# Making and storing the outputs of seven batches between the last two passes of a software-pipelined transformer kernel

## The reference

```python
x = x + tanh(g_xattn) * xattn(layernorm(x), ctx, ctx, Wq, bq, Wk, bk, Wv, bv, Wo, bo)   # 16 heads of 8
x = x + tanh(g_ffn) * stack(layernorm(x), ...)
# stack:
for i in range(6):
    x = attn_layer(shift_tokens(x), ...) + x     # 16 heads of 64, rotary, windows of 32 tokens and the 32 before
    x = ffn_layer(shift_tokens(x), ...) + x      # norm, 128 -> 2 x 341, a * gelu(gate), 341 -> 128
```

## Time and profile before

| what | us |
|---|---|
| median of 3 runs | 2186.88 (2184.47 to 2193.87) |
| the profiled execution, its own time | 2175.77 |
| its span, first to last instruction | 2173.8 |
| TensorE busy | 1993.4 (92% of the span) |
| VectorE busy | 1612.6 (74%) |
| ScalarE busy | 1092.6 (50%) |
| GpSimd busy | 891.2 (41%) |

### The profile page before, as it was taken

One profiled execution on the slowest core, in us unless ns is written; L12 is line 12 of the kernel. 1 busy time (PEld: TensorE's weight loads), 2 busy tenths in 40 slices (PEclk: granted clock), 3 DMA queues, 4 the chain that ended last, 5 costly groups with the idle time before them and its releaser, 6 DMA issues.

```text
span 2173.8 us, 84521 instructions
## 1 busy us (share of the span) xinstructions
PE 1993.4 (92%) x35280; PEld 1294.1 (60%) x35280; DVE 1612.6 (74%) x3316; ACT 1092.6 (50%) x1911; POOL 891.2 (41%) x1166
## 2 busy tenths in 40 slices
PE   6988987789999999999999999999999999999995
PEld 2333332456666666666766666767676766666763
DVE  5565563667878788787878787878787878787872
ACT  2333333345555555555555555656565646464643
POOL 1000000444545555455545454545454646463540
PEclk9999999899999999999999999999999999999996
DMA  1000100455556555556555565555655556554550
GB/s 61 5 5 10 53 0 1 69 85 82 84 82 123 93 84 84 83 111 104 86 80 89 97 108 90 89 79 96 114 96 87 84 84 112 103 86 81 84 83 21
DMA packets 73218, 166.72 MB, mean 77 GB/s; under 512 B 16592, under 2 KB 23504, under 8 KB 72272
## 3 DMA queue, kind: packets, MB, share of 16 engines
q0 software_dynamic: 36864, 100.71, 34.0%
q1 hardware_dynamic: 36320, 65.55, 11.8%
HBM read 20.45 MB, written 1.05 MB: 10 GB/s over the span
## 4 chain that ended last, share of the span: by engine, by line
PE 54%; DVE 18%; DMA 14%; issue 9%; POOL 4%; ACT 1%; POOLq 0%; DVEq 0%; SPq 0%; ACTq 0%
DMA big<-big 13%; PE ps L948 12%; PE ps L983 8%; PE ps L871 6%; PE ps L959 5%; PE ps L1020 4%; DVE big L770 4%; DVE big L767 3%; PE ps L1037 3%; POOL big L452 3%; PE ps L1007 3%; PE ps L892 2%; DVE big L801 2%; PE ps L876 2%; DVE big L788 2%
## 5 line engine op out<-in xcount | busy, mean ns | idle before, releaser
L452 POOL DMA_DIRECT2D big<-big x768 | 607.5, 1494 | 66.8 <-DVE big L770 56.1
L948 PE MATMUL ps<-big,wn_sb 128*128 128x256 f32 x1536 | 394.4, 393 | 25.5 <-issue 15.0
L520 ACT ACTIVATE big<-ps 128x512 f32<-128x512 f32 x384 | 229.1, 597 | 331.8 <-PE ps L948 325.4
L948 PEld LDWEIGHTS ps<-big,wn_sb 128*128 128x128 f32 x1536 | 273.2, 190 | 103.6 <-issue 46.5
L778 DVE TENSOR_TENSOR big<-big,ps 128x512 f32<-128x512 f32 x384 | 243.2, 682 | 103.3 <-DMA big<-big 52.4
L533 ACT ACTIVATE big<-ps 128x512 f32<-128x512 f32 x192 | 114.7, 598 | 371.3 <-PE ps L983 371.3
L783 DVE TENSOR_REDUCE top<-ps 128x8 f32<-128x512 f32 x192 | 123.3, 684 | 202.8 <-PE ps L1007 202.8
L767 DVE TENSOR_TENSOR big<-ps,tab 128x512 f32<-128x512 f32 x384 | 257.9, 682 | 9.3 <-ACT big L520 9.3
L770 DVE TENSOR_TENSOR big<-ps,tab 128x512 f32<-128x512 f32 x384 | 257.6, 681 | 0.0
L443 POOL TENSOR_TENSOR big<-big 128x512 f32<-128x512 f32 x96 | 121.9, 1270 | 294.2 <-ACT big L537 294.2
L1091 PE MATMUL ps<-big,wo_sb 128*128 128x256 f32 x768 | 213.1, 380 | 2.2 <-issue 2.2
(11 more groups left out here) (146 smaller groups left out, 3219.1 us busy)
## 6 DMA issues: line engine op xcount, KB each, us to landing
big<-big POOLq DMA_DIRECT2D x768, 128.0 KB, 4.9
big<-big SPq DMA_DIRECT2D x96, 256.0 KB, 3.9
big<-big SPq DMA_DIRECT2D x96, 192.0 KB, 4.0
wn_sb<-in_wn SPq DMA_DIRECT2D x6, 1024.0 KB, 9.1
wn_sb<-in_wn SPq DMA_DIRECT2D x6, 512.0 KB, 4.7
wo_sb<-in_wo SPq DMA_DIRECT2D x6, 512.0 KB, 3.4
w_sb<-in_w SPq DMA_DIRECT2D x6, 341.0 KB, 2.9
w_sb<-in_w SPq DMA_DIRECT2D x6, 192.0 KB, 2.9
```

Of the source, the lines that this page charges most:

```text
L452: eng.dma_start(rot[to:to + 32, at:at + 4, :], src[32 * r:32 * r + 32], accum_op=ALU.add).then_inc(added[i], 16)
L520: eng.activation(sq[:, two, :], ps[:, i % 2, :].rearrange("p (a t) -> p a t", a=2), ACT.Square).then_inc(sq_d, 1)
L948: mm = eng.matmul(ps[:, k % 2, a * T:a * T + T], wn_sb[:, u * P:u * P + P], sT, start=True, stop=True)
```

## The change

One helper, `outputs(first, last)`, holds the output steps of PE, ACT and DVE. It is called twice: for batches 0 to 6 between pass 48 and pass 49, and for batch 7 behind pass 49. `otok` grows from two buffers to eight, so the copies on ACT no longer wait for stores. The wait of DVE for `fx` becomes 48 (batch 6 added) in the first call and stays at 49 in the second. The loop on SP is the same but for the buffer that it reads.

```diff
-        otok = view(2 * 2 * P, 2, 2, P)
+        otok = view(B * 2 * P, B, 2, P)
...
             body(0, L * B, L, False, True, True, False)
+            if outputs:
+                outputs(0, B - 1)
             body(1, L * B + 1, L, False, False, True, False)
...
+            if outputs:
+                outputs(B - 1, B)
...
             body(L * B, False, True, True)
+            outputs(0, B - 1)
             body(L * B + 1, False, False, True)
+            outputs(B - 1, B)
...
-                eng.dma_start(o_tok[b], otok[:, b % 2, :, :]).then_inc(s_out[b % 2], 16)
+                eng.dma_start(o_tok[b], otok[:, b, :, :]).then_inc(s_out[b % 2], 16)
...
-                if b >= 2:
-                    eng.wait_ge(s_out[b % 2], 16 * (b // 2))
-                eng.activation(otok[:, b % 2, :, :], ps[:, b % 2, 0:T].rearrange("p (n d) -> p n d", n=NT),
-                               ACT.Copy).then_inc(ev_o, 1)
+                    eng.activation(otok[:, b, :, :], ps[:, b % 2, 0:T].rearrange("p (n d) -> p n d", n=NT),
+                                   ACT.Copy).then_inc(ev_o, 1)
...
-            eng.wait_ge(fx, L * B + FREE)
-            for b in range(B):
+            def outputs(first, last):
+                eng.wait_ge(fx, L * B - B + last + FREE)
+                for b in range(first, last):
```

More of the change, by code:

```diff
@@ L293, in seq, with pipeline @@
             return slice((b - n) % B, (b - n) % B + 1) if isinstance(b, int) else bass.ds(b - n, 1)
-        def pipeline(eng, body, layer_start=None, layer_second=None):
+        def pipeline(eng, body, layer_start=None, layer_second=None, outputs=None):
             def layer(l, first):
@@ L309, in pipeline, with passes @@
             body(0, L * B, L, False, True, True, False)
+            if outputs:
+                outputs(0, B - 1)
             body(1, L * B + 1, L, False, False, True, False)
-        def passes(eng, body):
+            if outputs:
+                outputs(B - 1, B)
+        def passes(eng, body, outputs):
             body(0, True, False, False)
@@ L564, in body @@
                         eng.preload_act_table_set("natural_log_exp_and_others")
-            pipeline(eng, body)
-            for b in range(B):
-                eng.wait_ge(tr_o, b + 1)
-                if b >= 2:
-                    eng.wait_ge(s_out[b % 2], 16 * (b // 2))
-                eng.activation(otok[:, b % 2, :, :], ps[:, b % 2, 0:T].rearrange("p (n d) -> p n d", n=NT),
-                               ACT.Copy).then_inc(ev_o, 1)
+            def outputs(first, last):
+                for b in range(first, last):
+                    eng.wait_ge(tr_o, b + 1)
+                    eng.activation(otok[:, b, :, :], ps[:, b % 2, 0:T].rearrange("p (n d) -> p n d", n=NT),
+                                   ACT.Copy).then_inc(ev_o, 1)
+            pipeline(eng, body, outputs=outputs)
         @block.vector
@@ L806, in body, with outputs @@
                         eng.tensor_tensor(xb, xb, ps[:, 2:3, T:2 * T], ALU.add).then_inc(x_d, 1)
-            pipeline(eng, body, layer_start, layer_second)
-            eng.wait_ge(fx, L * B + FREE)
-            for b in range(B):
-                eng.scalar_tensor_tensor(x1[:, b, :], xs[:, b, 1:T + 1], gates[:, 1:2], x1[:, b, :], ALU.mult,
-                                         ALU.add).then_inc(gx, 1)
+            def outputs(first, last):
+                eng.wait_ge(fx, L * B - B + last + FREE)
+                for b in range(first, last):
+                    eng.scalar_tensor_tensor(x1[:, b, :], xs[:, b, 1:T + 1], gates[:, 1:2], x1[:, b, :], ALU.mult,
+                                             ALU.add).then_inc(gx, 1)
+            pipeline(eng, body, layer_start, layer_second, outputs)
         @block.tensor
@@ L1098, in body, with outputs @@
                     steps[kind](i)
[L1100 to L1107, removed]
+            def outputs(first, last):
+                for b in range(first, last):
+                    eng.wait_ge(gx, b + 1)
+                    if b >= 2:
+                        eng.wait_ge(ev_o, b - 1)
+                    for n in range(NT):
+                        mm = eng.transpose(ps[:, b % 2, n * P:n * P + P], x1[:, b, n * P:n * P + P], ident)
+                    mm.then_inc(tr_o, 1)
+            passes(eng, body, outputs)
 def laid_out(inputs):
```

## The result

| | before | changed |
|---|---|---|
| median, first set of 5 runs each | 2186.88 us (2184.47 to 2193.87) | 2174.19 us (2169.36 to 2179.0) |
| ratio, 95% interval | | 0.9942 (0.992 to 0.9964) |
| the profiled execution's span | 2173.8 us | 2171.7 us |
| of it, from pass 48's last sum into the state to the end | 34.2 us | 28.9 us |

The median says 12.7 us faster, the two traces say 5.3 us in the part that the change can reach. The whole spans differ by 2.1 us only, since the changed kernel's profiled execution reached pass 48's last sum 3.2 us later (2142.84 against 2139.63).

The account below looks back on a forecast made before the run. PE, busy 92% in the untouched full passes, was put aside; stores that copies wait for fill the end. Tail 8.75 less delay 2.9 gives 5.85 us, so 2186.88 becomes 2181.0; range 2173 to 2188.

Parts of the forecast that it names:

- What the tail gives: Behind the last feed-forward only batch 7 is left, so the span ends at 2165.03 instead of 2173.8: 8.75 us.
- batch 0's way: Sum, transposes and copy, 2161.15 to 2162.80 in the trace before, taken as batch 7's path; then 2.23 us to the end.
- What pass 49 loses: Seven batches' transposes ahead of pass 49's first matmul on PE delay it 2.9 us, between 2.1 and 3.15 by clock.
- they start 0.40 apart: DVE's seven sums ahead of pass 49 follow each other at 0.40 us and take 2.9 us in all.
- the round trip over the banks: PE waits for ACT to empty a bank: 1.22 us per two batches at slow clock, 0.96 at full, setting PE's pace.
- The bounds given for the forecast's time: The forecast of 2181.0 us was given bounds of 2180.7 to 2181.9.
- Rival (c): POOL's copies hold DVE's sums up once or twice for 0.7 us: gain 4.45 us, 2182.4; chance 0.10.
- Rival (a): PE's clock stays up longer, up to pass 49's norm averages: chain 1.1 us late, gain 7.65 us, 2179.2; chance 0.18.
- rival (b): Full clock through all of pass 49, projections faster too: gain 12.1 us, 2174.8; chance 0.04.
- Rival (d): PE stops for code between 2141 and 2165, each costing 2.36 us; three make it slower, 2188.1; chance 0.04.
- The sum and its place in the time: Tail's 8.75 less pass 49's 2.9 is 5.85 us, taken from the median 2186.88: 2181.0 us; chance 0.62.
- the half per cent: About what a measurement can tell from no change; chances given: faster 0.13, same 0.83, slower 0.04.

Follow-up runs that it names:

- the idle transposes: Kernel before, outputs where they were, plus transposes that nothing reads in pass 49's waits; first matmul to sum 16.1 us, the whole end 30.3 us.
- the spread version: Changed kernel with the seven batches' steps put into waits inside pass 49, a PSUM bank each; ratio 0.9915, again 0.9944, against the kernel before.
- the three later sets: Changed kernel, unchanged, timed again in each set beside the kernel before on the same chip; ratios 0.9956, 0.9976 and 0.9972.

## Why the prediction was right or wrong

**What the tail gives.** Forecast 8.75 us, measured 8.7 (13.2 to 4.5), and 8.9 to 9.6 against the other three profiles of the kernel before, whose ends were longer. Right: the chain of waits had named the stores, and batch 0's way in the trace before was batch 7's way in the trace after. One thing in it was taken over unexamined, the store of 3.15 us. The sum came out because a landing of 3.1 to 4.0 us stands in every profile of the kernel before; with the same tail and no such landing, as under the idle transposes, the tail is 11.8 us, and only 7.3 of it could have been gained.

**What pass 49 loses.** Forecast 2.9 us with bounds of 2.1 and 3.15, measured 3.4 in three profiles of four and 2.9 in the fourth. The mechanism was right, the term mis-sized. The step "they start 0.40 apart" failed: the sums start 0.54 apart on average ((3.71 - 0.48) / 6), because two of them met POOL's copies, which put PE's third batch at 1.65 us behind its first instead of at 0.96. So at first DVE set PE's pace and not the round trip over the banks. The first transposes came 0.1 us earlier than assumed, and from the third batch on the rounds of 1.22 us were as worked out, which together makes 0.5 us more than forecast. In the fourth profile the clock held 1.5 us longer and gave the same 0.5 us back: that it meets the forecast of 2.9 us is luck.

The bounds given for the forecast's time, 2180.7 to 2181.9, don't follow from the delays of 2.1 and 3.15 us: those give 2180.2 and 2181.3.

**Rival (c) was part of the forecast's case.** It said that the copies hold the sums up once or twice by 0.7 us each. They did so twice, by 0.47 and 0.39 us (0.95 and 0.86 against 0.48), and the experiment with the sums behind the copies shows that the meeting causes it. On PE's third batch it came to 0.7 us, half of the 1.4 that the rival allowed. The Trainium skill, SBUF — State Buffer, section "SBUF: two separate sides", was read there in one direction only: that the copies would wait for the sums. The trace has both: one copy took 0.84 us for 0.72, two sums twice their time. A lock that is passed to and fro, one instruction each, agrees with that; the durations alone don't show the order in which it was held.

**The clock.** Rival (a) happened in part, in one profile of the changed kernel in four. In the third one the clock, at 0.50 for the last transposes, came back to 1.00 and fell again 3.5 us later; the norm's average (L1071) took 0.70 us in place of 1.22:

```profile
2146.00:2148.00 2.00, 0.70 (x2) 0.30 (x2) 0.00 (x0) 1.18 (x3) 0.00 (x0) 1.00 0.39 114
2146.37 0.70 PE L1071 MATMUL ps<-big,sel 128*128 128x256 f32 x2 [0.47 <-ACT big L553]
```

From its first matmul to its sum pass 49 took 17.9 us there, against 18.6 in the other three. With a bank for each batch the clock stayed up through both groups of the norm, and the pass took 17.6. In all of these it was down again at the first up projections, which took 2.04 us or more. The full clock in the projections, which is rival (b)'s gain, came about in the spread version, where the same transposes stand in the waits of the pass, and in part with the idle ones. A full clock through the whole pass came about nowhere. The Trainium skill, TensorE: Matmul & The Clock Gate, section "Part 1: The HAM clock gate", says that activity releases the throttle. That is borne out by the spread version and by the idle transposes, with 14.1 and 16.1 us for what takes 17.6 to 18.7 in all other profiles.

**Rival (d), stops of PE for code.** The stops are real, up to 4.2 us in one pass 48 and none in another, but none of the 14 profiles has one in pass 49 or behind it. So what the rival feared didn't happen. That they are fetches of code is argued, not shown: they stand in straight code, and packets of the instruction queue q8 go with them. In the four profiles without a stop the second of these packets behind pass 47's sum comes 9.5 to 10 us after it, in the ten others at 12 us or later. Whether the stops come from late packets or the packets are late from the stops isn't shown.

**The sum and its place in the time.** Forecast 5.85 us, found 5.8 in the ends of the traces and 6.8 (1.9 either way) in the pooled means. That the ends agree so closely is luck: in the mean of four profiles each, pass 49 began 3.3 us later for 2.9 forecast, and the tail gave 9.1 us for 8.75, the landings of the later profiles being longer. The first set showed 12.7, beyond the half per cent to which the text had given 0.13; the three later sets gave 0.4, 0.2 and 0.3%, all within it. The working knew the spread, 9.4 us among three runs against an effect of 6, and widened the range for it. The time fell in that range, but a time of one set was never going to confirm the sum. The end of the trace could, since it is nearly free of that scatter.

## What to carry to other kernels

What a tail can give is read from the way of the batch that stays, not from the waits in its chain: with no copy waiting for a store it still took 10.1 of 13.2 us. Its work can go where engines wait for one another, but every engine runs in order: put it behind the link that the next engine waits for, not ahead of it. Here seven batches in front of the last pass cost 3.4 of the 8.7 us that they saved (2.9 in one profile of four), and inside its waits nothing, with some 4 us more from TensorE's clock.

Where an effect is smaller than the scatter of a run, compare the stretch that the change can reach in several traces, and let identical kernels run against each other before a difference elsewhere is explained. A pattern of 27 to 33 us against 31 to 35 us in eleven profiles didn't hold in the fourteenth.

## What the hardware showed that was not expected

- DVE sums with two operands in SBUF and POOL's copies lengthen each other: 0.95 and 0.86 us for 0.48, and 0.84 for 0.72. The trace shows this as duration, not as a wait, and with the sums behind the copies it is gone.
- The span up to pass 47's last sum varied from 2102.9 to 2125.4 us, and pass 48, with the same code, from 27.5 to 35.4 us, with stops of PE of 0.2 to 2.9 us that no engine releases.
- A store of 128 KB lands 1.8 to 1.9 us after its issue, also with seven issued within 3.7 us. In the five profiles where one packet of the instruction queue falls among the stores, some of those issued about then take 2.8 to 4.0 us.
- Idle transposes in the waits of a latency-bound stretch made it about 2 us shorter, since they brought TensorE's clock back to 2.4 GHz for part of it.
